# The first weight-tile loads asked for by ScalarE instead of SyncE

## The chip, the cores and the metric

The kernel runs on one core of one Trainium2 chip. The time is that of one execution on the device in microseconds (us), the median of several runs; lower is better.

## The reference, cut to what matters

Eight batches of x (256 x 1024, float32) pass through four residual layers. Layer 0 is a dense product with a low-rank addition chosen by a label, layer 1 a quantisation by thresholds, layer 2 a dense product with a weight chosen by an adapter number, and layer 3 a low-rank product.

```python
x = x + _L0_cond_ref(x, itok_B_0_2, L0_cond_W, L0_cond_lora_A, L0_cond_lora_B_w)   # x @ W.T + low rank
x = x + _L1_cond_ref(x, condB_thresholds, condB_deltas, condB_zeropoints)          # quantise
x = x + _L2_cond_ref(x, L2_cond_weight, itok_B_3_7)                                # x @ w[adapter].T
x = x + _L3_cond_ref(x, L3_cond_A, L3_cond_B, itok_B_3_7)                          # rank 16
```

## The kernel before, in words

A batch of x lies in SBUF as 128 partitions x 2048 floats: eight blocks k of 256 columns. The weight of layer 0 has eight tiles o of 128 x 1024, taken in the order 0, 2, 1, 3, 4, 6, 5, 7; n counts the place in this order. Layer 0 reaches float32 precision in three products of rounded parts: ScalarE writes the rounded part (`x_hi`, `w0_hi`), VectorE the rest (`x_lo`, `w0_lo`), and TensorE computes hi by hi, hi by lo and lo by hi (`main0`, L945). Ahead of that GpSimd adds the identity to the diagonal block of each weight tile (L456), which is how the residual comes in.

Every engine has one fixed list of instructions; semaphores set the order between them. Loads are asked for by SyncE, in the order of its list. Each ask takes its sequencer about 0.4 us, and the transfer lands later.

What matters here is the start, for batch 0. TensorE first runs ten products of the identity with itself (`WARM = 10`, L1131), which give nothing that is used. Then `first_tiles` multiplies the first two weight tiles with x as they were loaded (`plain0`, L953), without the split into parts, so that TensorE has work before the parts are ready. Each `plain0` is one 128 x 128 block of a weight tile by one 128 x 256 block of x, and it shows as two records in the trace. For this start the loads are cut small: x in four quarters (L352, 256 KB each; two blocks k in each) and the weight tiles n = 0 and n = 1 in two halves each (L356, 256 KB each; four blocks k in each). SyncE asks in this order: x quarter 0, tile 0 half 0, x quarter 1, the labels, the adapter numbers, tile 1 half 0, x quarter 2, tile 0 half 1, x quarter 3, tile 1 half 1, and then the whole tile n = 2 (L279, 512 KB). After that SyncE waits for the labels and goes on with the low-rank factor of the label (L275), tile n = 3 and the rest.

TensorE takes them in this order:

```python
pe.wait_ge(x_quarter_loaded[0], 16); pe.wait_ge(w0_half_loaded[0], 16)
plain0(0, 1, start=True); plain0(0, 0)
pe.wait_ge(x_loaded[0], 16)                  # quarter 1
plain0(0, 2); plain0(0, 3)
pe.wait_ge(w0_half_loaded[1], 16)
plain0(1, 0, start=True); plain0(1, 1); plain0(1, 3); plain0(1, 2)
pe.wait_ge(w0_loaded[0], 16); pe.wait_ge(x_quarter_loaded[1], 16)
plain0(0, 4); plain0(0, 5)
pe.wait_ge(x_loaded[1], 16)                  # quarter 3
plain0(0, 6); plain0(0, 7)
pe.wait_ge(w0_loaded[1], 16)                 # then plain0(1, 4) to plain0(1, 7)
```

`plain0(0, 0)` and `plain0(1, 2)` also wait for GpSimd's addition to that block. The products with a low-rank factor (L1001) follow, and then `main0` for tile n = 2, which needs that tile loaded, added to (L456), rounded (L490) and split (L724).

ScalarE's list begins with a wait for the identity and an ACTIVATE of one column (L684), ahead of which the trace has the load of the activation tables. Then it rounds x quarter 0, quarter 1, tile 0 half 0, quarter 2, tile 0 half 1, quarter 3, tile 1, and the two halves of tile 2. It asks for no transfer.

Of the kernel before, what the change touches and what calls it, by code (L numbers as in the profile page):

```python
# [19 lines left out]
CW = BW // 4  # L20
# [33 lines left out]
ORDER = (0, 2, 1, 3, 4, 6, 5, 7)  # L54
# [6 lines left out]
def build(nc, x, labels, adapters, thresholds, deltas, zeropoints, w0, a0, b0, w2, b3, b3_wide, a3, out):  # L61
    with ExitStack() as ctx:
# [6 lines left out]
        def sem(name):  # L69
            return ctx.enter_context(nc.semaphore(name))  # L70
# [50 lines left out]
        w0_loaded = [sem(f"w0_loaded{o}") for o in range(T)]  # L121
        x_loaded = [sem(f"x_loaded{h}") for h in range(2)]
        x_quarter_loaded = [sem(f"x_quarter_loaded{h}") for h in range(2)]
        w0_half_loaded = [sem(f"w0_half_loaded{n}") for n in range(2)]
# [80 lines left out]
        def w0_stage(n):  # L205

            if n >= 2 * CANDS:
                return quant[:, n % 2 * T * P:(n % 2 + 1) * T * P]
            return cand[:, (n // 2 + 1) % CANDS, n % 2 * T * P:(n % 2 + 1) * T * P]
# [57 lines left out]
        def _(sp):  # L267
# [10 lines left out]
            def load_w0(n):  # L278
                sp.dma_start(w0_stage(n), w0[ORDER[n]]).then_inc(w0_loaded[n], 16)  # L279
# [70 lines left out]
            def load_first_x(i, loaded):  # L350
                cols = slice(i * CW, (i + 1) * CW)
                sp.dma_start(x_raw[:, cols], x[0, :, cols]).then_inc(loaded, 16)  # L352

            def load_first_w0(n, h, loaded):
                cols = slice(h * CW, (h + 1) * CW)
                sp.dma_start(w0_stage(n)[:, cols], w0[ORDER[n], :, cols]).then_inc(loaded, 16)  # L356

            load_first_x(0, x_quarter_loaded[0])
            load_first_w0(0, 0, w0_half_loaded[0])
            load_first_x(1, x_loaded[0])  # L360
            sp.dma_start(label_ids[:, :], labels.rearrange("(a n) -> a n", a=1)).then_inc(ids_loaded, 16)
            sp.dma_start(adapter_ids[:, :], adapters.rearrange("(a n) -> a n", a=1)).then_inc(ids_loaded, 16)
            load_first_w0(1, 0, w0_half_loaded[1])
            load_first_x(2, x_quarter_loaded[1])
            load_first_w0(0, 1, w0_loaded[0])
            load_first_x(3, x_loaded[1])
            load_first_w0(1, 1, w0_loaded[1])
            load_w0(2)
            sp.wait_ge(ids_loaded, 2 * 16)
            load_a0(0)  # L370
# [107 lines left out]
        def _(act):  # L478
# [190 lines left out]
            def quantise(u):  # L669
# [4 lines left out]
                for j in range(1, G):  # L674
# [5 lines left out]
                        candidate(u, j + 1)  # L680
                    between(u, j)

            act.wait_ge(ident_ready, 1)
            act.activation(magnitude[:, 0:1], ident[:, 0:1], ACT.Abs)  # L684
            split_first_x(0)
# [529 lines left out]
```

## Time and profile before

| | |
|---|---|
| median of 3 runs | 456.52 us (456.33 to 457.02) |
| the profiled execution, its own time | 456.12 us |
| its span, first to last instruction | 454.2 us |
| TensorE busy | 446.5 us, 98% of the span |
| VectorE busy | 422.3 us, 93% |
| ScalarE busy | 357.7 us, 79% |
| mean granted TensorE clock over the span | 1.000 |

In the trace, PE is TensorE's matmul, PEld its weight load, DVE VectorE, ACT ScalarE, POOL GpSimd, and SPq SyncE's sequencer. L352 is line 352 of the kernel. Times of rows are microseconds from the start of the span.

### The profile page before, as it was taken

How to read it: one execution, taken by the hardware profiler on the slowest of the kernel's cores; microseconds unless marked ns; L12 is line 12 of the kernel's file. 1: busy time of each engine (PE TensorE's matmuls, PEld its weight loads, DVE VectorE, ACT ScalarE, POOL GpSimd, SP SyncE). 2: the span in 40 equal slices, each digit the busy share in tenths (PEclk: the TensorE clock that was granted, in tenths of full speed). 3: DMA queues.
4: the chain of work that ended last, by engine and by line, in shares of the span. 5: the costliest groups of instructions: out<-in, count | busy, mean ns of one | idle time of the engine just before them, and what ended most of it. 6: DMA issues, size and time to landing. Idle time of an engine off the chain costs nothing.

```text
span 454.2 us, 7843 instructions
## 1 busy us (share of the span) xinstructions
PE 446.5 (98%) x3094; PEld 408.0 (90%) x3094; DVE 422.3 (93%) x402; ACT 357.7 (79%) x331; POOL 42.6 (9%) x54
## 2 busy tenths in 40 slices
PE   8999999999999999999999999999999999999995
PEld 7899999989998999889998999989999989998784
DVE  4699999999999998999899998999969999999993
ACT  5699999998699768977799775997568958585740
POOL 3300010002200010000101010110100101000000
PEclk9999999999999999999999999999999999999999
DMA  7973463496358835786459835486353615578022
GB/s 252 326 292 105 94 168 78 127 255 185 82 198 219 255 83 152 206 227 205 82 193 224 253 83 152 152 213 171 68 186 130 173 60 125 165 222 312 1 93 92
DMA packets 35640, 75.62 MB, mean 167 GB/s; under 512 B 3988, under 2 KB 14100, under 8 KB 34836
## 3 DMA queue, kind: packets, MB, share of 16 engines
q1 hardware_dynamic: 30708, 61.50, 40.1%
q0 software_dynamic: 4896, 13.63, 17.2%
q8 instruction: 24, 0.39, 0.3%
q14 instruction: 12, 0.10, 0.1%
HBM read 53.10 MB, written 8.39 MB: 135 GB/s over the span
## 4 chain that ended last, share of the span: by engine, by line
PE 77%; DVE 15%; issue 6%; ACT 1%; DVEq 0%; POOL 0%; POOLq 0%; ACTq 0%
PE l_ps L945 35%; PE l_ps L1046 23%; PE l_ps L1058 6%; DVE quant L808 5%; DVE cand L782 4%; PE l_ps L1074 3%; PE bx_ps L1001 2%; PE l_ps L953 2%; PE bx_ps L1093 2%; PE l_ps L987 1%; DVE cand L790 1%; DVE x L760 1%; PE l_ps L1131 1%; DVE x L859 1%; PE l_ps L1123 1%
## 5 line engine op out<-in xcount | busy, mean ns | idle before, releaser
L1046 PE MATMUL l_ps<-x,w_sb 128*128 128x256 f32 x672 | 150.2, 380 | 0.0
L808 DVE COPY_PREDICATED quant<-mask,cand 128x2048 f32<-128x2048 int8 (+2 forms) x77 | 146.5, 1903 | 0.4
L1046 PEld LDWEIGHTS l_ps<-x,w_sb 128*128 128x128 f32 x672 | 126.1, 190 | 18.2 <-issue 2.1
L589 ACT ACTIVATE cand<-x,inv_delta 128x2048 f32<-128x2048 f32 (+2 forms) x88 | 134.4, 1528 | 9.9 <-DVE quant L802 8.0
L599 ACT ACTIVATE mask<-magnitude,thr_bias 128x2048 fp8e5<-128x2048 f32 (+2 forms) x77 | 117.5, 1526 | 8.8 <-DVE quant L808 8.2
L782 DVE TENSOR_SCALAR cand<-cand,delta 128x2048 f32<-128x2048 f32 (+2 forms) x88 | 87.9, 999 | 7.3 <-ACT cand L589 7.1
L790 DVE TENSOR_SCALAR cand<-cand,lower,upper 128x2048 f32<-128x2048 f32 (+2 forms) x88 | 93.4, 1061 | 0.4
L945 PE MATMUL l_ps<-x_hi,w_hi 128*128 128x256 f32 x496 | 82.8, 289 | 0.0
L945 PE MATMUL l_ps<-x_hi,w_lo 128*128 128x256 f32 x496 | 79.7, 283 | 0.0
L945 PE MATMUL l_ps<-x_lo,w_hi 128*128 128x256 f32 x496 | 79.7, 283 | 0.0
L945 PEld LDWEIGHTS l_ps<-x_hi,w_hi 128*128 128x128 f32 x496 | 68.7, 191 | 5.0 <-issue 3.7
L945 PEld LDWEIGHTS l_ps<-x_hi,w_lo 128*128 128x128 f32 x496 | 68.4, 192 | 0.0
L945 PEld LDWEIGHTS l_ps<-x_lo,w_hi 128*128 128x128 f32 x496 | 68.4, 192 | 0.0
L464 POOL DMA_DIRECT2D w_lo<-w_edge x28 | 28.4, 1013 | 233.5 <-ACT w_lo L568 233.5
L537 ACT ACTIVATE x<-l_ps 128x1024 f32<-128x1024 f32 x16 | 16.3, 1017 | 24.7 <-DVE x L760 15.7
L1058 PE MATMUL l_ps<-x_hi,w_hi 128*128 128x256 f32 x112 | 27.7, 329 | 0.0
L760 DVE TENSOR_TENSOR x<-l_ps,x 128x512 f32<-128x512 f32 x32 | 22.3, 706 | 2.0 <-PE l_ps L1074 1.8
L1058 PE MATMUL l_ps<-x_lo,w_hi 128*128 128x256 f32 x112 | 22.5, 282 | 0.0
L1058 PE MATMUL l_ps<-x_hi,w_lo 128*128 128x256 f32 x112 | 22.4, 282 | 0.0
L1058 PEld LDWEIGHTS l_ps<-x_hi,w_hi 128*128 128x128 f32 x112 | 19.3, 190 | 1.4
L559 ACT ACTIVATE bx_split<-bx_ps 128x256 fp32r<-128x256 f32 x8 | 3.0, 379 | 20.9 <-PE bx_ps L1100 13.0
L802 DVE SCALAR_TENSOR_TENSOR quant<-magnitude,sorted_thr,cand 128x2048 f32<-128x2048 f32 (+2 forms) x11 | 19.4, 1765 | 0.0
(89 smaller groups left out, 403.4 us busy)
## 6 DMA issues: line engine op xcount, KB each, us to landing
w_sb<-w SPq DMA_DIRECT2D x60, 384.0 KB, 3.7
out<-x SPq DMA_DIRECT2D x32, 256.0 KB, 2.3
x_raw<-x SPq DMA_DIRECT2D x14, 512.0 KB, 5.7
w_edge<-w SPq DMA_DIRECT2D x28, 256.0 KB, 3.5
w_lo<-w_edge POOLq DMA_DIRECT2D x28, 256.0 KB, 4.7
x_lo<-x_raw POOLq DMA_DIRECT2D x6, 1024.0 KB, 8.5
x<-a SPq DMA_DIRECT2D x7, 512.0 KB, 3.4
cand<-w SPq DMA_DIRECT2D x4, 512.0 KB, 8.5
```

The lines of the kernel that those rows point to most:

```text
L464: pool.dma_start(split_pair(w2_lo, b, q), raw_edges(q), accum_op=ALU.add).then_inc(w2_added[q], 16)
L537: act.activation(x2[:, b % SLOTS, h * HW:(h + 1) * HW], l0_ps[:, h, :], ACT.Copy).then_inc(x0_done, 1)
L589: act.activation(cand[:, c % CANDS, 0:n], x2_unit(u), ACT.Identity, bias=ROUND, scale=inv_delta[:, k:k + 1]).then_inc(rounded, 1)
L599: act.activation(mask[:, m % MASKS, 0:n], magnitude[:, 0:n], ACT.Relu, bias=thr_bias[:, k:k + 1], scale=STEEP, saturate=False).then_inc(ma ...
L760: dve.tensor_tensor(x3[:, cols], l2_bank(b, q), x2[:, b % SLOTS, cols], ALU.add).then_inc(x3_done, 1)
L782: dve.tensor_scalar(t, t, -ROUND, delta[:, k:k + 1], ALU.add, ALU.mult).then_inc(scaled, 1)
L790: dve.tensor_scalar(t, t, lower[:, k:k + 1], upper[:, k:k + 1], ALU.max, ALU.min).then_inc(clipped, 1)
L802: dve.scalar_tensor_tensor(y, magnitude[:, 0:n], sorted_thr[:, G - 1:G], t, ALU.is_gt, ALU.mult)\
L808: dve.copy_predicated(y, mask[:, m % MASKS, 0:n].bitcast(I8), t).then_inc(merged, 1)
L945: nc.tensor.matmul(dst, w[:, o, k * P:(k + 1) * P], v[:, b % 2, k * S:(k + 1) * S], start=(o % 2 == 0 and v is x_hi and w is w0_hi and k = ...
L1046: last = nc.tensor.matmul(l2_bank(b, q)[:, i * S:(i + 1) * S], w2_block(b, o, k), x2[:, b % SLOTS, k * S:(k + 1) * S], start=(i == 0 and k ...
L1058: last = nc.tensor.matmul(l2_bank(b, q)[:, i * S:(i + 1) * S], w[:, k * P:(k + 1) * P], v[:, k * S:(k + 1) * S], start=False, stop=(i == 1 ...
```

## The change

The four loads of weight tiles 0 and 1 leave SyncE's list and stand at the head of ScalarE's, ahead of its wait for the identity, in the order tile 0 half 0, tile 1 half 0, tile 0 half 1, tile 1 half 1. Sizes, destinations and semaphores stay. SyncE now asks for x quarter 0, x quarter 1, the labels, the adapter numbers, x quarter 2, x quarter 3, tile 2, and goes on as before.

```diff
@@ SyncE
             load_first_x(0, x_quarter_loaded[0])
-            load_first_w0(0, 0, w0_half_loaded[0])
             load_first_x(1, x_loaded[0])
             sp.dma_start(label_ids[:, :], labels.rearrange("(a n) -> a n", a=1)).then_inc(ids_loaded, 16)
             sp.dma_start(adapter_ids[:, :], adapters.rearrange("(a n) -> a n", a=1)).then_inc(ids_loaded, 16)
-            load_first_w0(1, 0, w0_half_loaded[1])
             load_first_x(2, x_quarter_loaded[1])
-            load_first_w0(0, 1, w0_loaded[0])
             load_first_x(3, x_loaded[1])
-            load_first_w0(1, 1, w0_loaded[1])
             load_w0(2)
@@ ScalarE
+            def load_first_w0(n, h, loaded):
+                cols = slice(h * CW, (h + 1) * CW)
+                act.dma_start(w0_stage(n)[:, cols], w0[ORDER[n], :, cols]).then_inc(loaded, 16)
+
+            load_first_w0(0, 0, w0_half_loaded[0])
+            load_first_w0(1, 0, w0_half_loaded[1])
+            load_first_w0(0, 1, w0_loaded[0])
+            load_first_w0(1, 1, w0_loaded[1])
             act.wait_ge(ident_ready, 1)
             act.activation(magnitude[:, 0:1], ident[:, 0:1], ACT.Abs)
```

## Rows read from the trace of the kernel before

**Rows 1.** The page: busy time, share of the span, instructions; the chain by engine.
```profile
PE 446.5 (98%) x3094; PEld 408.0 (90%) x3094; DVE 422.3 (93%) x402; ACT 357.7 (79%) x331; POOL 42.6 (9%) x54
PE 77%; DVE 15%; issue 6%; ACT 1%; DVEq 0%; POOL 0%; POOLq 0%; ACTq 0%
```

**Rows 2.** Chain that ended last, its first pieces: start us, us, what, records.
```profile
1.54 4.64 PE l_ps L1131 x20
6.17 7.47 PE l_ps L953 x32
13.64 1.00 PE bx_ps L1001 x16
14.64 3.06 PE l_ps L945 x24
```

**Rows 3.** TensorE by line: durations ns min/median/max, first and last start, shape.
```profile
L1131 PE MATMUL l_ps<-ident x20: 421/421/580, 1.5 to 5.8; 128*128 128x128 f32 x20
L953 PE MATMUL l_ps<-x_raw,cand x32: 379/379/694, 6.0 to 13.3; 128*128 128x256 f32 x32
```

**Rows 4.** Timeline, TensorE's matmuls and weight loads around the first data.
```profile
5.97 1.10 PE L953 MATMUL l_ps<-x_raw,cand 128*128 128x256 f32 x2
7.43 1.03 PE L953 MATMUL l_ps<-x_raw,cand 128*128 128x256 f32 x4
5.87 0.29 PEld L953 LDWEIGHTS l_ps<-x_raw,cand 128*128 128x128 f32 x1
6.90 0.30 PEld L953 LDWEIGHTS l_ps<-x_raw,cand 128*128 128x128 f32 x2 [0.53 <-POOL cand L456]
7.22 0.19 PEld L953 LDWEIGHTS l_ps<-x_raw,cand 128*128 128x128 f32 x1
```

**Rows 5.** Timeline, SyncE's asks: start us, us of its sequencer.
```profile
0.76 0.39 SPq L352 DMA_DIRECT2D x_raw<-x  x1
1.20 0.42 SPq L356 DMA_DIRECT2D cand<-w  x1
1.67 0.42 SPq L352 DMA_DIRECT2D x_raw<-x  x1
...
2.79 0.36 SPq L356 DMA_DIRECT2D cand<-w  x1
...
4.60 0.45 SPq L356 DMA_DIRECT2D cand<-w  x1
5.09 0.43 SPq L279 DMA_DIRECT2D cand<-w  x1
```

**Rows 6.** The lines of the first loads: from ask to landing.
```profile
DMA to landing us min/median/max: 4.3/4.9/6.0
DMA to landing us min/median/max: 4.4/4.8/5.8
```

**Rows 7.** Timeline, who starts when its load has landed: ScalarE and GpSimd.
```profile
0.75 1.28 ACT L684 ACT_TABLE_LOAD   x1 [0.75 <-PEq L1207]
2.04 0.20 ACT L684 ACTIVATE magnitude<-ident 128x1 f32<-128x1 f32 x1
5.18 0.63 ACT L495 ACTIVATE x_hi<-x_raw 128x512 fp32r<-128x512 f32 x1 [2.94 <-DMA x_raw<-x]
6.43 0.63 ACT L495 ACTIVATE x_hi<-x_raw 128x512 fp32r<-128x512 f32 x1 [0.62 <-DMA x_raw<-x]
5.84 1.01 POOL L456 TENSOR_TENSOR cand<-cand,ident 128x128 f32<-128x128 f32 x1 [2.88 <-DMA cand<-w]
7.18 0.91 POOL L456 TENSOR_TENSOR cand<-cand,ident 128x128 f32<-128x128 f32 x1 [0.34 <-DMA cand<-w]
```

**Rows 8.** Timeline, the way of tile 2 to the first `main0`.
```profile
11.95 1.36 POOL L456 TENSOR_TENSOR cand<-cand,ident 128x128 f32<-128x128 f32 x1 [3.85 <-DMA cand<-w]
13.34 1.15 ACT L490 ACTIVATE w_hi<-cand 128x512 fp32r<-128x512 f32 x2 [1.60 <-POOL cand L456]
14.57 0.74 PE L945 MATMUL l_ps<-x_hi,w_hi 128*128 128x256 f32 x4
```

More of the change, by code:

```diff
@@ L352, in load_first_x @@
                 sp.dma_start(x_raw[:, cols], x[0, :, cols]).then_inc(loaded, 16)
-            def load_first_w0(n, h, loaded):
-                cols = slice(h * CW, (h + 1) * CW)
-                sp.dma_start(w0_stage(n)[:, cols], w0[ORDER[n], :, cols]).then_inc(loaded, 16)
             load_first_x(0, x_quarter_loaded[0])
-            load_first_w0(0, 0, w0_half_loaded[0])
             load_first_x(1, x_loaded[0])
```

## Prediction

> **What bounds the kernel now.** I read the page first. TensorE is busy 98% of the span, and the chain that ended last runs through its matmuls for 77% [rows 1]. The change touches only the first five microseconds of asks, so the next view is that chain in order of time, at its start. It goes from the warm-up products straight into the first products with data, from these into the low-rank products and then into `main0`: four pieces, each beginning where the last one ended, and no load and no other engine between them [rows 2]. So at the start TensorE is the bound, and the question is what sets the moment of its first product with data, and whether any later load is close to holding it up.
>
> The first question is answered by two rows. The last warm-up record begins at 5.8, after 20 records from 1.5 on, so (5.8 - 1.5) / 19 = 0.22 us from one to the next [rows 3]. The first record with data begins at 5.97 [rows 4]. That is one such step behind the last warm-up record. The half tile that it needs landed at 5.84 (GpSimd, which waits for the same semaphore, starts then) and quarter 0 of x at 5.18 [rows 7]. So the warm-up ends just when the data is there: the warm-up fills the wait, and it would go on to about 5.95 if the data came sooner.
>
> **How fast TensorE works there.** A warm-up record has 128 columns and takes a step of 0.22 us. A record of L953 has 256 columns, twice the work; from 7.43 to the last at 13.3 there are 28 of them, so a step of (13.3 - 7.43) / 27 = 0.217 us [rows 3, 4]. The mean granted clock is shown as 1.000, but by these steps the engine worked at its lower level (1.2 GHz) during the warm-up and at 2.4 GHz from about 7.2 on. The four records from 5.97 to 7.43 took 1.46 us where four steps of 0.217 make 0.87.
>
> **The change part by part.** *Four asks leave SyncE.* One costs 0.42 plus the gap to the next, 0.47 from start to start (1.20 to 1.67) [rows 5]. So what follows comes earlier: x quarter 1 by 0.47 (asked at 1.20), quarter 2 and quarter 3 by two and three asks, tile 2 by four, 1.9 us (from 5.09 to 3.2). SyncE's sequencer holds nothing up here, so by itself this is worth nothing.
>
> *Four asks come to ScalarE.* At 0.47 each they fill its sequencer for 1.9 us. If they start at 0.75, when ScalarE's list starts now [rows 7], they end at 2.6; the table load of 1.28 then ends at 3.9 and the ACTIVATE of one column, 0.20, at 4.1. The next thing on ScalarE waits for x quarter 0, which landed at 5.18 [rows 7]. 1.1 us of cover is left; without it each microsecond would push the rounded parts, and behind them VectorE's. Cost: 0.
>
> *Where the table load stands.* No row shows it with asks ahead of it. Now it starts at 0.75, while the ACTIVATE behind it waited for the identity (ready at 1.5), so it is not held by that wait. It may come behind the four asks, where its ACTIVATE is, or at the head of the list, as now. I take behind them; the other order is a rival below. By the Trainium skill (ScalarE: Activation LUTs, section "Step-by-step: what each stage is for") the compiler places the load right before the ACTIVATE that needs it. The trace agrees as far as it goes: its row bears the line of that ACTIVATE, L684.
>
> *When the halves and quarters land.* The landings now, from the asks plus [rows 6], or from who starts on them [rows 7]: x quarter 0 at 5.18, tile 0 half 0 at 5.84, quarter 1 at 6.43, tile 1 half 0 at 7.18, quarter 2 near 8.2, tile 0 half 1 near 8.8, quarter 3 near 10.0, tile 1 half 1 at 4.60 + 6.0 = 10.6. They come one by one, some 0.7 to 0.9 us apart, while the asks were only 0.47 apart: from about 3 us on it is the transfers that limit, not the asks. So asking with two sequencers brings no more bytes per microsecond. It changes the order: with two streams served side by side, a quarter of x and a half tile move together, and each pair is there when its second member is there now: pair 1 at 5.84, pair 2 at 7.18, pair 3 at 8.8, pair 4 at 10.6.
>
> *When TensorE needs them.* It loads the weights of `plain0(0, 2)` at 7.22 [rows 4] and then one `plain0` takes two steps, 0.43. Quarter 1 is needed at 7.22. Tile 1 half 0 comes two products later, 8.1; quarter 2 and tile 0 half 1 six later, 9.8; quarter 3 eight later, 10.7; tile 1 half 1 ten later, 11.5. Against the pairs that leaves 0.04 for quarter 1 (0.79 now), 0.9 for tile 1 half 0, 1.0, 0.1 for quarter 3 (0.7 now), and 0.9. Nothing is late by this, but two margins have shrunk to nearly none. The bounds for each: 0, and, if everything lands one place later in the present order, 0.8 us late. I take 0.1 for both together, since the sum says in time by a hair and the first asks will be nearer together than now.
>
> *What an earlier landing can give.* At the first product nothing, since the warm-up stands there until about 5.95. `plain0(0, 0)` waited for GpSimd's addition, but the weight load idled 0.53 [rows 4] while the matmul records before it were still running at the lower clock: two of them from 5.97 at twice 0.217 end near 6.85, the addition ended at 6.85 (5.84 + 1.01). Gain: 0 to 0.05.
>
> *Tile 2 and what is behind it.* The bytes ahead of tile 2 are the same 2 MB, so it lands near 11.95 as now; GpSimd, ScalarE and TensorE follow at 11.95, 13.34 and 14.57 [rows 8]. The first rounded half is ready at 13.34 + 0.6 = 13.9, 0.6 us ahead of TensorE. Cost 0, and up to that much delay would stay hidden. GpSimd's queue holds nothing else that this moves.
>
> By the Trainium skill (DMA: Bandwidth & Descriptors, section "Issuing engines are not separate DMA queues") asks from several engines end up on the same 16 DMA engines and only the sequencer's time is saved. The landings above, 0.7 to 0.9 apart behind asks 0.47 apart, agree. By that rule alone the sum would be 0.
>
> **The sum.** Start of data products 0, thin margins +0.1, everything else 0. The profiled execution took 456.12 (span 454.2 and 1.9 around it), so 456.2 for it; the median of the runs stands 0.40 above that execution. Forecast 456.6.
>
> **The rivals.** *The table load stays first.* Then tile 0 half 0 is asked for at 0.75 + 1.28 = 2.03 instead of 1.20, and with 4.4 to 4.7 us to landing [rows 6] it lands at 6.4 to 6.7. The warm-up no longer covers it: the first product comes 0.5 to 0.8 us later. Half of that may come back, as fewer records then fall in the slow stretch before 7.2. Time: +0.3 to +0.8, 456.8 to 457.3. For it: the table load doesn't wait for the identity now. Against it: the line it bears.
>
> *The asks slow each other.* If both sequencers share what generates the transfers, the two lists come out as one at the present pace, and the change does nothing: 456.5. For it: the asks are nearly all the same 0.42, whatever was queued.
>
> *A hole in TensorE's work delays the clock (slower).* The clock rose only after 5.7 us of unbroken work, 1.54 to about 7.2 [rows 2, 4]. A hole of some tenths between 5.95 and 7.2, from half 0 or quarter 1 being late, may set that back. Each microsecond longer at the lower level costs half of one; all 5.7 again would cost 2.8, with the hole itself 0.6: 459.9. It decides from about 1.0 us of delay on, a rise 1 to 2 us later. Against it: the chain shows no hole there now, and the hole would be short.
>
> *Faster.* If the pairs landed a full microsecond earlier and the slow stretch from 5.97 to 7.43 shrank to 0.87, the gain would be 0.6: 455.9. More is not to be had before 14 us, because the warm-up's length is fixed, and nothing in it depends on a load.
>
> **How the numbers follow.** Forecast as summed 0.55, asks slow each other 0.12, table load first 0.20, delayed clock 0.08, faster 0.05. Within 0.2%, 0.9 us, is about what a measurement of this kernel can't tell from no change; the runs shown differ by 0.7. The first three cases all lie in it: with most of their weight 0.85. Slower by more: 0.10, from the delayed clock and the tail of the table case. Faster by more: 0.05. The range takes in the forecast, the table case and the spread of the runs: 455.9 to 457.4.
>
> **What would show it.** Right: in the timeline of ScalarE four asks from 0.75, the table load from 2.6, the first data matmul again at 5.97 and the piece of L953 in the chain again 7.5 us long; quarter 0 of x rounded later than 5.18, near 5.8, and quarter 1 near 7.2. Wrong: a first data matmul later than 6.1, a wait of TensorE between 7 and 12, or `main0` beginning later than 14.6 with a wait for tile 2. The prediction falls if the step of 0.22 lasts beyond 7.5.

## The result and the profile after

The changed kernel takes 457.74 us (13 executions, 457.13 to 459.38) against 456.65 for the kernel before in the same rounds (13 executions, 456.11 to 457.33). The ratio is 1.0024, 95% interval 1.0017 to 1.0032: slower by 1.1 us. How far such an interval can be trusted is seen from r5, a copy of the kernel before, which came out at 1.0013: a difference of 0.1% can't be told from none here. The 0.24% came again in r1. The profiled execution is the slowest of the thirteen, 459.38 with a span of 457.3; a second profile of the same kernel (below) is an ordinary one, 457.83 with a span of 455.8.

The chain that ended last, at its start, in the changed kernel's profiled execution (start us, us, what), answers to [rows 2]:

```profile
0.75 0.40 SPq L352
1.15 0.06 issue
1.20 7.50 DMA x_raw<-x
8.70 0.04 issue
8.74 8.00 PE l_ps L954 x28
16.74 1.00 PE bx_ps L1002 x16
17.74 3.06 PE l_ps L946 x24
```

Before, it began with the warm-up. Now it begins with a load: the one that SyncE asks for at 1.20, x quarter 1, which takes 7.5 us. Behind it stand 28 of the 32 records of the first products, so the hole is after `plain0(0, 0)`, where `plain0(0, 2)` waits for that quarter.

ScalarE, GpSimd and TensorE in the timeline of the same execution, which answers to [rows 4, 5, 7, 8]:

```profile
0.75 2.21 ACTq L678 DMA_DIRECT2D cand<-w  x4
2.99 1.28 ACT L685 ACT_TABLE_LOAD   x1 [2.99 <-issue]
5.38 0.63 ACT L487 ACTIVATE x_hi<-x_raw 128x512 fp32r<-128x512 f32 x1 [0.89 <-DMA x_raw<-x]
8.72 0.63 ACT L487 ACTIVATE x_hi<-x_raw 128x512 fp32r<-128x512 f32 x1 [2.71 <-DMA x_raw<-x]
...
3.27 1.32 SPq L279 DMA_DIRECT2D cand<-w  x1
...
5.25 0.45 POOL L448 TENSOR_TENSOR cand<-cand,ident 128x128 f32<-128x128 f32 x1 [2.29 <-DMA cand<-w]
8.50 0.45 POOL L448 TENSOR_TENSOR cand<-cand,ident 128x128 f32<-128x128 f32 x1 [2.79 <-DMA cand<-w]
13.09 0.45 POOL L448 TENSOR_TENSOR cand<-cand,ident 128x128 f32<-128x128 f32 x1 [4.14 <-DMA cand<-w]
...
5.83 1.03 PE L954 MATMUL l_ps<-x_raw,cand 128*128 128x256 f32 x4
8.74 8.00 PE L954 MATMUL l_ps<-x_raw,cand 128*128 128x256 f32 x28 [1.88 <-DMA x_raw<-x]
17.67 0.74 PE L946 MATMUL l_ps<-x_hi,w_hi 128*128 128x256 f32 x4
```

The asks and the table load stand as forecast: four asks from 0.75, the table load behind them. The first pair lands at 5.25 (tile 0 half 0, by GpSimd's start) and 5.38 (x quarter 0). The second pair lands at 8.50 and 8.72, where tile 1 half 0 and quarter 1 landed at 7.18 and 6.43 before [rows 7].

The same execution in stretches of one microsecond: length, busy time and number of each engine, then PEclk, the granted clock, DMA share and GB/s.

```profile
8.00:9.00 1.00, 0.26 (x1) 0.26 (x2) 0.00 (x0) 0.28 (x1) 0.45 (x1) 1.00 1.07 408
9.00:10.00 1.00, 1.00 (x4) 0.80 (x4) 0.62 (x2) 0.87 (x2) 0.00 (x0) 0.55 1.03 411
10.00:11.00 1.00, 1.00 (x4) 0.82 (x3) 0.68 (x2) 0.45 (x1) 0.00 (x0) 0.50 1.01 378
11.00:12.00 1.00, 1.00 (x3) 0.75 (x3) 0.79 (x2) 1.00 (x3) 0.00 (x0) 0.50 1.02 408
12.00:13.00 1.00, 1.00 (x5) 0.84 (x4) 1.00 (x2) 1.00 (x2) 0.00 (x0) 0.75 1.12 260
13.00:14.00 1.00, 1.00 (x7) 0.87 (x6) 0.91 (x2) 0.59 (x2) 0.45 (x1) 1.00 0.98 205
```

Behind the hole the granted clock is 0.50 of full for some three and a half microseconds, that is 1.2 GHz, and the stretches count 3 to 5 records where the last one, back at 1.00, counts 7 (a record that reaches over a border is counted on both sides of it, so the counts are too high as a rate). That isn't so in every execution. In the second profile of the same kernel the clock stays at 1.00, and the 28 records take 6.31 instead of 8.00:

```profile
1.21 7.40 DMA x_raw<-x
8.61 0.04 issue
8.65 6.31 PE l_ps L954 x28
14.96 1.00 PE bx_ps L1002 x16
15.96 3.07 PE l_ps L946 x24
```

So there are two parts of the loss, and the second profile has only the first. In the first profile `plain0(0, 2)` starts at 8.74 instead of 7.43 [rows 4], +1.3; its 28 records take 8.00 instead of 13.64 - 7.43 = 6.2 [rows 2, 4], +1.8; the first `main0` comes at 17.67 instead of 14.57 [rows 8], +3.1, and the span is 3.1 longer. In the second profile +1.2 and +0.1 make +1.3 at the first `main0` (15.89), and the span is 1.6 longer; the other 0.3 comes at tile n = 4, whose 24 records take 3.17 us in r1 and 2.88 before. The profile of [rows 1] is of a fast execution: against r5, whose first `main0` starts at 15.02, that of r1 is 0.9 later.

### The profile page after: what moved, and what is told of

Same layout as the page of the kernel before. It is cut to its first block, busy times and chain, and to the rows that moved or that the text cites. A ratio compares the mean times of both kernels' runs of the same rounds, so it can differ in the third digit from the quotient of the medians.

```text
span 457.3 us, 7843 instructions
## 1 busy us (share of the span) xinstructions
PE 447.6 (98%) x3094; PEld 408.6 (89%) x3094; DVE 422.2 (92%) x402; ACT 356.9 (78%) x331; POOL 41.6 (9%) x54
## 3 DMA queue, kind: packets, MB, share of 16 engines
q10 hardware_dynamic: 576, 1.05, 0.7%
## 4 chain that ended last, share of the span: by engine, by line
PE 75%; DVE 15%; issue 6%; DMA 2%; ACT 1%; DVEq 0%; SPq 0%; ACTq 0%
PE l_ps L946 35%; PE l_ps L1047 23%; PE l_ps L1059 6%; DVE quant L809 5%; DVE cand L783 4%; PE l_ps L1075 3%; PE bx_ps L1002 2%; PE l_ps L954 2%; DMA x_raw<-x 2%; PE bx_ps L1094 2%; PE l_ps L988 1%; DVE cand L791 1%; DVE x L761 1%; DVE x L860 1%; PE l_ps L1124 1%
## 5 line engine op out<-in xcount | busy, mean ns | idle before, releaser
L946 PE MATMUL l_ps<-x_hi,w_hi 128*128 128x256 f32 x496 | 82.8, 289 | 0.0
L946 PE MATMUL l_ps<-x_hi,w_lo 128*128 128x256 f32 x496 | 79.7, 283 | 0.0
L946 PE MATMUL l_ps<-x_lo,w_hi 128*128 128x256 f32 x496 | 79.6, 283 | 0.0
L946 PEld LDWEIGHTS l_ps<-x_hi,w_hi 128*128 128x128 f32 x496 | 68.7, 191 | 5.0 <-issue 3.7
L946 PEld LDWEIGHTS l_ps<-x_hi,w_lo 128*128 128x128 f32 x496 | 68.4, 192 | 0.0
L946 PEld LDWEIGHTS l_ps<-x_lo,w_hi 128*128 128x128 f32 x496 | 68.3, 191 | 0.0
```

The source lines that it names most:

```text
L946: nc.tensor.matmul(dst, w[:, o, k * P:(k + 1) * P], v[:, b % 2, k * S:(k + 1) * S], start=(o % 2 == 0 and v is x_hi and w is w0_hi and k = ...
```

## The experiments

All kernels were run in five rounds beside the kernel before, the last in three. The number of executions of each is in the table. Every time is that of the kernel and its ratio to the kernel before in the same rounds. "Quarter 1 lands" is the start of its rounding by ScalarE; in r4, r10 and r12 this follows on another rounding without a gap, so there the quarter had landed by then, perhaps earlier.

| kernel | quarter 1 lands | first `main0` | span | median us (executions) | ratio, 95% interval |
|---|---|---|---|---|---|
| before, profile of [rows 1] | 6.43 | 14.57 | 454.2 | 456.65 (13) | |
| r5 before, again | 6.52 | 15.02 | 454.5 | 456.87 (11) | 1.0013, 1.0004 to 1.0022 |
| changed | 8.72 | 17.67 | 457.3 | 457.74 (13) | 1.0024, 1.0017 to 1.0032 |
| r1 changed, again | 8.63 | 15.89 | 455.8 | 457.83 (9) | 1.0025, 1.0013 to 1.0036 |
| r2 small asks behind quarter 3 | 8.49 | 17.44 | 457.0 | 458.04 (8) | 1.0033, 1.0023 to 1.0043 |
| r3 filler in the hole | 8.34 | 15.61 | 455.1 | 457.79 (7) | 1.0027, 1.0016 to 1.0038 |
| r4 one half on ScalarE | 6.25 | 13.96 | 454.2 | 455.98 (11) | 0.9985, 0.9977 to 0.9994 |
| r10 the same, again | 6.11 | 14.53 | 454.1 | 456.18 (12) | 0.9996, 0.9987 to 1.0006 |
| r6 two halves on ScalarE | 7.98 | 15.24 | 454.8 | 456.83 (11) | 1.0009, 1.0000 to 1.0018 |
| r7 ScalarE's last two asks later | 7.71 | 15.59 | 455.1 | 457.22 (11) | 1.0012, 0.9999 to 1.0025 |
| r8 SyncE holds quarter 2 back | 7.46 | 16.41 | 456.4 | 458.37 (5) | 1.0051, 1.0037 to 1.0065 |
| r9 both holds | 6.55 | 18.46 | 458.0 | 459.74 (6) | 1.0065, 1.0050 to 1.0079 |
| r11 late wait, loads as before | 6.78 | 16.55 | 456.1 | 458.87 (6) | 1.0062, 1.0037 to 1.0086 |
| r12 one list, ScalarE's | 6.75 | 14.84 | 454.9 | 457.09 (10) | 1.0004, 0.9991 to 1.0018 |

Span less start of the first `main0` is 439.5 to 440.2 in every row of this table (454.2 - 14.57 = 439.6; 457.3 - 17.67 = 439.6; 458.0 - 18.46 = 439.5). The whole effect of the change, and of each variant, arises ahead of the first `main0`; nothing behind it gives it back, and at most 0.7 is added. The rows that stand out, r1 with 439.9, r8 with 440.0, r12 with 440.1 and r4 with 440.2, lose this at one place: the 24 records of tile n = 4 take 3.17, 3.34, 3.28 and 3.34 us there, and 2.88 before. What stands behind it in r4 is told below.

**r1, the changed kernel again.** No edit.

> The changed kernel once more, since the profiled execution of it (459.38) was the slowest of its thirteen. Theory A (x quarter 1 lands late behind two interleaved streams, TensorE stands still before its third product, and that hole is most of the cost): the median is again 1.0 to 1.3 above the kernel before, and an ordinary execution shows a hole of 1 to 1.5 us between the fourth and the fifth record with data, at little loss of clock. Theory B (the hole is short and it is the lower clock behind it that costs): the hole is under 0.7 us and at least 0.5 us of the loss is in matmuls at twice the step. Theory C (the loss is behind 14 us, by tile 2 or the low-rank factor being late): the first main0 begins near 14.6 and a wait stands behind it.

The median is 1.3 above the kernel before, and the hole is 2.0 us long (the wait shown for TensorE ahead of the 28 records) with no loss of clock. Its length is more than A gave; but part of it is not loss, since the clock had risen at 5.0 here and the four records ahead of it were done the earlier. What counts is the start of `plain0(0, 2)`, 8.65 against 7.43. B and C fell: the clock stayed at 1.00 and the work from there to `main0` was only 0.1 longer.

**r2, the small asks moved.**

```diff
             load_first_x(1, x_loaded[0])
-            sp.dma_start(label_ids...); sp.dma_start(adapter_ids...)
             load_first_x(2, x_quarter_loaded[1])
             load_first_x(3, x_loaded[1])
+            sp.dma_start(label_ids...); sp.dma_start(adapter_ids...)
             load_w0(2)
```

> The changed kernel with SyncE's two small asks (labels, adapter numbers) moved behind x quarter 3. They stand behind quarter 1 in the list, so theory A (quarter 1 is late by the other stream's bytes) expects quarter 1 as late as before and the same time within 0.3 us. A rival (the small transfers take turns of their own on a DMA engine and delay the x stream) expects quarters 2 and 3 earlier and 0.5 us or more back.

Quarter 1 lands at 8.49, 0.1 to 0.2 earlier, and the time is no lower. The small transfers are not the cause.

**r3, filler in the hole.**

```diff
                 plain0(0, 0)
+                for i in range(8):
+                    nc.tensor.matmul(l3_ps[:, 0:P], ident[:, :], ident[:, :], start=True, stop=True)
```

> The changed kernel with eight more products of the identity behind plain0(0, 0), that is in the hole; they take 8 x 2 records of 128 columns, about 1.7 us at the higher clock. Nothing else changes. Theory A: quarter 1 lands as late, so the time stays within 0.3 us of the changed kernel, or grows by what the filler is longer than the hole. Theory B: the clock never falls, so 0.5 us or more comes back, and the executions spread less.

The filler takes 1.95 us in the hole and the median stays, 457.79 against r1's 457.83. So in most executions it is the late start of `plain0(0, 2)` that costs, and the clock costs nothing. The fall of the clock, seen in the profiled executions of the changed kernel and of r2, is a second, occasional cost: among the 30 executions of the changed kernel, r1 and r2, four have a mean granted clock of 0.995 and take 459.1 to 459.4; with the filler none of 7 does (457.12 to 458.42). Seven are too few to say that the filler prevents it.

**r4 and r10, one half only.**

```diff
@@ SyncE
-            load_first_w0(0, 0, w0_half_loaded[0])
@@ ScalarE, at the head
+            act.dma_start(w0_stage(0)[:, 0:CW], w0[ORDER[0], :, 0:CW]).then_inc(w0_half_loaded[0], 16)
```

> The kernel before with only tile 0 half 0 asked for by ScalarE; the other three halves stay in SyncE's list in the old order. Theory A: only one half tile competes with the x stream, quarter 1 lands no later than 6.9, TensorE has no hole, and the time is that of the kernel before within 0.3 us. If an ask by ScalarE costs by itself (a second queue in use, ScalarE held up), the time is 0.5 us or more above.

> The kernel with only tile 0 half 0 on ScalarE's queue once more. It measured 0.9985 of the kernel before, while a copy of the kernel before measured 1.0013 of it, so a single comparison is not enough. If the gain is real, the ratio is again 0.9975 to 0.9995; if it was chance, it is 0.9995 to 1.0015. Quarter 1 lands at 6.2 to 6.6 in either case.

An ask on ScalarE's queue costs nothing by itself: quarter 1 has landed by 6.25 and 6.11, no later than before. r4's time was 0.6 below the kernel before, outside the 0.3 that was expected, but this was not repeated: 0.9985, then 0.9996, which is in the range named for chance, with r5, a copy of the kernel before, at 1.0013. It stays open whether this version is faster by up to 0.1%. The two traces differ by the clock. In r4 the 32 records of the first products take 7.07 us from 5.85; in r10, the same kernel, 7.64 from 5.96; before, 7.67 from 5.97. r4's are at the higher clock from the first one on, the other two only from about 7.2, so the 0.6 by which r4's first `main0` is ahead of [rows 8] is nearly all of it the clock's, and r10's (14.53 against 14.57) isn't ahead. In r4 0.6 was lost again at tile n = 4:

```profile
9.20 9.26 DMA cand<-w
18.45 0.07 issue
18.52 1.31 POOL cand L455
19.83 0.02 issue
19.86 1.07 ACT w_hi L482
20.92 0.14 issue
21.06 3.34 PE l_ps L945 x24
```

This is r4's chain, in order of time: the load asked for at 9.20 lands at 18.46, GpSimd, ScalarE and then TensorE follow without slack. A front that is half a microsecond shorter can run into the next load. It isn't a matter of the shorter front alone, since r1, r8 and r12 lose 0.3 to 0.5 at the same tile.

**r5, the kernel before again.** No edit.

> The kernel before once more, for a second trace of it: the one read for the prediction was among its fastest executions. With one half moved to ScalarE the time fell by 0.6, which the prediction's reading (the warm-up fills the wait up to 5.95 whatever the loads do) does not allow. Theory D: the clock rises at a different moment in each execution; where it rises during the warm-up, this ends before tile 0 half 0 has landed, and TensorE has a hole ahead of its first product with data. Then this trace shows warm-up records at half the step and a first product that starts with the landing at about 5.8, behind a gap. If D is false, the first product begins one step behind the last warm-up record again.

Its first product starts at 5.98, 0.23 behind the last warm-up record, as in [rows 3, 4], so this trace doesn't show D. Others do. In r3 the clock rose at about 4.6, during the warm-up; this ended early, and the first product (5.54) started behind tile 0 half 0's landing at 5.48. In r11 tile 0 half 0 landed at 6.19 and TensorE waited 0.61 for it. The moment of the rise moves between executions, from 4.6 (r3) to about 7.5 (r5), under the same warm-up. The prediction's statement that the warm-up covers the landing holds for an execution like the one it read, not for all.

**r6, two halves on ScalarE.**

```diff
@@ SyncE
-            load_first_w0(0, 0, w0_half_loaded[0])
-            load_first_w0(1, 0, w0_half_loaded[1])
@@ ScalarE, at the head
+            act_first_w0(0, 0, w0_half_loaded[0])
+            act_first_w0(1, 0, w0_half_loaded[1])
```

> The kernel before with tile 0 half 0 and tile 1 half 0 asked for by ScalarE, the two second halves in SyncE's list as before. If it is the number of bytes asked for on the second queue that makes quarter 1 late (theory A), quarter 1 lands between the one-half kernel (6.3) and the changed one (8.6 to 8.7), at 7.0 to 7.8, and the time is between theirs, 456.0 to 457.8. If the lateness comes from the deep queue alone (four asks outstanding on ScalarE's), quarter 1 lands by 6.6 and the time is that of the one-half kernel.

Quarter 1 lands at 7.98, 0.2 later than the range named, and between one half and four, so it is not only a queue four asks deep. The time, 456.83, lies in its range; with 1.0009 it can't be told from the copy of the kernel before (1.0013).

**r7, r8, r9: who takes the bandwidth.** r7 moves ScalarE's last two asks behind its first rounding; r8 makes SyncE wait for quarter 1 ahead of its ask for quarter 2; r9 does both.

```diff
@@ ScalarE (r7, r9)
-            load_first_w0(0, 1, w0_loaded[0])
-            load_first_w0(1, 1, w0_loaded[1])
             act.wait_ge(ident_ready, 1)
             act.activation(magnitude[:, 0:1], ident[:, 0:1], ACT.Abs)
             split_first_x(0)
+            load_first_w0(0, 1, w0_loaded[0])
+            load_first_w0(1, 1, w0_loaded[1])
@@ SyncE (r8, r9)
+            sp.wait_ge(x_loaded[0], 16)
             load_first_x(2, x_quarter_loaded[1])
```

> The changed kernel with ScalarE's third and fourth asks (tile 0 half 1, tile 1 half 1) moved behind its first rounding, so that they are asked for at about 5.5 and 6.0 instead of 1.66 and 2.14. If bytes asked for early on ScalarE's queue delay quarter 1, it lands 0.5 us or more earlier than 8.6, and TensorE's hole there shrinks by as much; a new hole of up to 0.5 may open at tile 0 half 1, needed near 9.8. If the delay is from the second queue being in use at all, the landing stays at 8.5 or later.

> The changed kernel with a wait in SyncE's list for quarter 1's landing ahead of the ask for quarter 2, so that up to then only two quarters and the small transfers are asked for on SyncE's queue. If the x stream's own later loads take bandwidth from quarter 1, it lands 0.5 us or more earlier than 8.6; if only ScalarE's stream does, it stays at 8.5 or comes slightly earlier. Quarters 2 and 3 and tile 2 come late in either case, so the total is expected above the changed kernel's, 458 to 461.

> Both holds at once: ScalarE's third and fourth asks stand behind its first rounding, and SyncE waits for quarter 1's landing before it asks for quarter 2. Up to quarter 1's landing only four transfers of 256 KB are asked for, two on each queue, besides the two small ones. Each hold alone brought quarter 1 from 8.6 to 7.7 and to 7.5. If what delays quarter 1 is all the bytes asked for behind it, on either queue, it lands at 7.2 or earlier, where the pair rule of the prediction puts it. If a fixed cost of the second queue is part of it, it stays at 7.4 or later. The total is above the changed kernel's in either case, since quarters 2 and 3 come late.

Quarter 1 lands at 7.71, 7.46 and 6.55. Each hold brings about one microsecond, both bring 2.1. With only four transfers asked for until 5.4, the second pair is even 0.6 ahead of the prediction's 7.18: ScalarE's timeline in r9 has both roundings early.

```profile
5.37 0.63 ACT L488 ACTIVATE x_hi<-x_raw 128x512 fp32r<-128x512 f32 x1 [2.21 <-DMA x_raw<-x]
5.37 0.82 ACTq L679 DMA_DIRECT2D cand<-w  x2
6.55 0.63 ACT L488 ACTIVATE x_hi<-x_raw 128x512 fp32r<-128x512 f32 x1 [0.56 <-DMA x_raw<-x]
```

What it costs is later. In r7 TensorE stands for another 0.34 us at 10.94, where tile 0 half 1 has just landed. In r8 and r9 quarters 2 and 3 come late (in r9 at 11.4 and 13.2) and TensorE stands again, so the times are 458.37 and 459.74; in r9's profile the clock falls too (12 records take 4.34 us, in r8's 2.86), and three of its six executions have a mean granted clock of 0.994 or 0.995. No hold is a way out.

How much had moved when the second pair was there is in one line for each kernel: a stretch from 1.00 to that landing; its length is the second number, its GB/s the last one. In this order they are the kernel before, r1, r8 and r9.

```profile
1.00:7.18 6.18, 5.64 (x23) 5.11 (x24) 1.37 (x5) 2.61 (x5) 2.29 (x8) 1.00 0.70 208
```

```profile
1.00:8.63 7.63, 5.11 (x24) 4.61 (x24) 1.29 (x4) 2.12 (x3) 1.87 (x9) 1.00 0.80 244
```

```profile
1.00:7.46 6.46, 5.81 (x24) 5.29 (x24) 1.28 (x4) 2.12 (x4) 1.89 (x9) 1.00 0.75 235
```

```profile
1.00:6.55 5.55, 5.01 (x23) 4.96 (x24) 1.12 (x4) 2.12 (x3) 1.98 (x9) 1.00 0.64 192
```

Length times rate over 0.262 MB, one such load, gives the loads' worth of bytes moved when four of them had landed: before, 6.18 x 208 = 1.29 MB or 4.9 loads; r1, 1.86 MB or 7.1; r8, 1.52 MB or 5.8, with six asked for; r9, 1.07 MB or 4.1, with four asked for until 5.4. The transfers are not slower in the changed kernel: by 7.18 r1 had moved 1.31 MB, the kernel before 1.29. But three loads' worth that nobody needs yet come ahead of the last bytes of the second pair, where one list brought one.

The view of the transfers by queue shows whose bytes these are. q10 is ScalarE's queue (in all it moves 1.05 MB, its four loads), q1 SyncE's; the second number is MB. First r1 from 1.00 to 7.18, when by the prediction the second pair lands, then from 1.00 to 8.63, when it was there:

```profile
q1 hardware_dynamic: 328, 0.61, 38.8%
q10 hardware_dynamic: 383, 0.70, 36.0%
```

```profile
q1 hardware_dynamic: 483, 0.89, 42.0%
q10 hardware_dynamic: 527, 0.97, 38.5%
```

Neither queue was starved by the other. At 7.18 each had moved more than two loads' worth (0.52 MB), and still neither had its second load complete; these were complete at 8.50 (tile 1 half 0) and 8.63 (quarter 1), and by then ScalarE's queue had moved 3.7 loads' worth and SyncE's 3.4. So on both queues bytes of later loads moved ahead of the rest of the second one.

**r11, the hole without the change.** All asks as before; TensorE waits earlier for what it waits for anyway.

```diff
                 pe.wait_ge(x_loaded[0], 16)
+                pe.wait_ge(w0_loaded[0], 16)
                 plain0(0, 2)
                 ...
-                pe.wait_ge(w0_loaded[0], 16)
                 pe.wait_ge(x_quarter_loaded[1], 16)
```

> The kernel before, all asks by SyncE, but TensorE waits ahead of plain0(0, 2) also for tile 0 half 1, which lands at 8.8 to 9.0 (it waits for it six products later anyway). So TensorE gets the hole of the changed kernel without the change. If the hole is all of the loss, plain0(0, 2) starts near 8.9, the first main0 near 15.9 and the time is 457.6 to 458.2, the changed kernel's; some executions may be 1 to 1.6 higher where the clock falls behind the hole. If the changed kernel loses time elsewhere too, this one stays below 457.4.

The median is 458.87, 0.7 above the range. Tile 0 half 1 landed at 9.2 in its trace, later than the 8.8 to 9.0 reckoned with, and `plain0(0, 2)` started at 9.34. The three executions whose mean granted clock is 0.999 or 1.000 take 457.76, 457.90 and 458.13, in the range; in the other three it is 0.993 to 0.995 and they take 459.61 to 461.38. The clock fell in half of the executions here, in four of 30 of the changed kernel, r1 and r2, to judge by the mean granted clock. The span less the start of `main0` is again 439.5. A late `plain0(0, 2)` alone is thus enough for a loss of this kind and size; the moved asks need nothing beside it. The miss in size is the clock's, which falls more often here; what decides how often is open.

**r12, one list again, on the other queue.**

```diff
@@ SyncE
-            (the eight first loads)
             sp.dma_start(label_ids...); sp.dma_start(adapter_ids...)
+            sp.wait_ge(x_quarter_loaded[0], 16)
             load_w0(2)
@@ ScalarE, at the head
+            (the eight first loads, in the order of the kernel before)
```

> All eight first loads in one list again, in the order of the kernel before, but ScalarE's; SyncE asks for the small transfers and, once quarter 0 has landed, for tile 2 and on as before. If lateness comes from two queues with asks outstanding side by side, quarter 1 lands at 6.3 to 6.8 as when SyncE asks for all, and TensorE has no hole of over 0.3 us before its fifth record with data. If ScalarE's queue is slower by itself, quarter 1 lands at 7.2 or later. ScalarE's sequencer is now busy with eight asks and the table load until about 6, so its first rounding is late by 0.5 to 1 us; the total may be the kernel before's or up to 1 us above.

```profile
0.75 0.38 ACTq L678 DMA_DIRECT2D x_raw<-x  x1
1.16 0.46 ACTq L682 DMA_DIRECT2D cand<-w  x1
1.65 0.45 ACTq L678 DMA_DIRECT2D x_raw<-x  x1
...
4.80 1.28 ACT L693 ACT_TABLE_LOAD   x1 [4.80 <-issue]
6.09 0.20 ACT L693 ACTIVATE magnitude<-ident 128x1 f32<-128x1 f32 x1
```

ScalarE's timeline shows seven asks of 0.38 to 0.46, as SyncE's [rows 5], and an eighth of 0.71. Quarter 1, asked for at 1.65, is rounded at 6.75, right behind quarter 0, and tile 1 half 0 lands at 7.49 (7.18 before), when 6.49 x 231 = 1.50 MB or 5.7 loads' worth had moved. ScalarE's queue is not slower, and TensorE has no hole. The time is that of the kernel before, 1.0004, although ScalarE starts its rounding only at 6.2; a rounding a microsecond late costs nothing that can be measured here. The stretch up to 7.49:

```profile
1.00:7.49 6.49, 5.95 (x24) 5.68 (x25) 1.23 (x5) 2.68 (x5) 1.74 (x8) 1.00 0.75 231
```

A rival is left untested. Two lists also bring the asks forward: the last of the eight is made at 2.75 in the changed kernel, at 4.60 before and at 4.06 in r12. No run splits the list and keeps the old pace, so how much of the lateness comes from two queues and how much from later loads being asked for sooner isn't separated.

## Why the prediction was wrong, point by point

**What bounds the start, TensorE and nothing else: right for before.** The chain after begins with a load instead, which is the change of bound that the prediction asked about and denied.

**The asks that leave SyncE, those that come to ScalarE, the table load: right.** Four asks of 0.40 to 0.82 from 0.75, the table load at 2.99, the ACTIVATE done at 4.5, and x quarter 0 at 5.38. Cost 0. The rival in which the table load stays first fell with this trace, and so did the one in which the asks slow each other so much that the two lists come out as one: the first two asks of each engine run side by side from 0.75, SyncE's in 0.40 and 0.44 us, ScalarE's in 0.40 and 0.45.

**When the halves and quarters land: the step that failed.** The prediction said that "with two streams served side by side, a quarter of x and a half tile move together, and each pair is there when its second member is there now: pair 1 at 5.84, pair 2 at 7.18". Pair 1 came at 5.38. Pair 2 came at 8.72 and 8.63, 1.5 later. The step took for granted that, with the rate unchanged, the bytes of the second pair would be the next to move. The rate was right (1.31 MB in r1 by 7.18, 1.29 before), the order was not. r1's bytes by queue and r6 to r9 show in its place that, with later loads asked for early on both queues, bytes of these move ahead of the rest of the second pair, which is complete only after 7.1 loads' worth of bytes instead of 4.9 (5.7 in r12); with four loads asked for (r9) it is complete after 4.1, and at 6.55. Its bound, "one place later in the present order, 0.8 us late", was too near as well; the landing was 1.4 to 1.5 behind the need at 7.22. The prediction also misread its rows in saying that the landings now come 0.7 to 0.9 apart: from 5.18 to 10.6 they are 0.6 to 1.2 apart. No term hangs on it.

By the Trainium skill (DMA: Bandwidth & Descriptors, section "Why a DMA increments its semaphore by 16 and not by 1") a load is spread over 16 DMA engines that finish independently, and only the full count says that all has landed. That fits a load waiting for its slowest share while other engines are already at later loads; by it alone the order of asks need not be the order of landings. The views here don't tell one DMA engine from another, so which shares are late, and why this goes so much further with two lists (7.1 loads' worth) than with one (4.9 and 5.7), stays open.

**Thin margins, +0.1: mis-sized, with the step above.** The term measured +1.2 to +1.3 (start of `plain0(0, 2)` at 8.65 and 8.74 against 7.43). The prediction had named the margin that gave way, 0.04 for quarter 1.

**The clock rival: half right.** It expected a hole of some tenths to delay the rise. The clock had risen before the hole, and behind a hole of about 2 us it fell in some executions, which costs another 1.7 (28 records in 8.00 instead of 6.31). That made the slowest executions, not the median. That the slowest of the thirteen, 459.38, is near this rival's 459.9 is chance, since its sum was another one. In r6, with a hole of 1.14 us, and r7, with two of 0.79 and 0.34, none of 22 executions shows the fall.

**Tile 2 and what is behind it: right in effect.** Its addition started at 13.09 and 13.25 instead of 11.95, later by more than forecast, but TensorE was later too, and nothing waited there: the chain runs from L954 through L1002 into L946 without a wait.

**The sum.** The median was forecast at 456.6 and came out at 457.74, 1.1 more, and the one term put at 0.1 that measured 1.2 to 1.3 makes up for it. The range ended at 457.4. Even the late bound of the landings, 0.8 in place of 0.1, would only have given 457.3, since it too was taken from rows with a single list.

## What to carry to other kernels

In these runs a list of loads on one queue also kept their order of arrival. Splitting it over two queues added no bandwidth where the transfers were already the limit, and it let later loads overtake the one that was needed next: its landing went from 6.4 to 8.7 us while the bytes per microsecond stayed the same (208 GB/s up to 7.18 before, 206 and 212 in the two profiles after). Before moving asks, take for each load the moment of need and ask what is outstanding on both queues then, not only what stands ahead of it in its own list; one ask moved left the landing where it was, two made it 1.5 us later. A loss at the front of a kernel that its matmuls fill passes whole into the time, and it can be read off the start of the first steady product.

## What the runs showed of the hardware that was not expected

- Some asks become slower when many are outstanding. ScalarE's fourth took 0.82, 0.85 and 0.88 us in the changed kernel, r1 and r2, its first two 0.40 and 0.45. SyncE's for tile 2 varies: 1.32 in the profiled execution, 0.54 in r1, 0.36 in r2, 0.43 before [rows 5]. It isn't special to two full queues, since the eighth ask on ScalarE's in r12 took 0.71 and SyncE's last half tile in r10 0.77, 0.45 before. No run shows a cost of it in time.
- The first rise of TensorE's clock, to judge by the steps between records, came anywhere from 4.6 to about 7.5 us under the same warm-up, while the granted clock was shown as 1.00 throughout. An early rise ends the warm-up before the first half tile is there (r3 and r11, where TensorE then waits 0.61 us); a late one makes the first products slow. r4 and r5, with rises near 5.8 and 7.5 and no hole, have their first `main0` at 13.96 and 15.02, and this 1.1 us is of the size of the spread of the kernel before (456.11 to 457.33).
